# Four graph layers on one core: a shared pool of PSUM banks, seven units, scores in three row groups, low halves of P on GpSimd

## The reference, cut to what matters

```
x = layernorm(x + L0(x, adj))   # 12-head attention, scores + beta*adj, masked where adj is 0
x = layernorm(x + L1(x, adj))   # 2 inner layers: u = h (W h)^T for two W, exp, times adj, @ (h W_lin), layernorm, relu
x = layernorm(x + L2(x, adj))   # 2 inner layers: softmax(h h^T) * adj, three projections, upper/diagonal/lower, layernorm, relu
x = layernorm(x + L3(x, adj))   # 12-head attention with adj as bias, then an output projection
# attention: P = softmax(q k^T * scale + bias) per head of 32 columns, out = P v
```

## Time and profile before

| what | value |
|---|---|
| median of 3 runs | 3090.86 us (3088.84 to 3092.55) |
| the profiled execution, its own time | 3095.68 us |
| span of its trace, first to last instruction | 3093.9 us |
| mean granted clock of PE | 0.979 of full speed |
| PE busy | 2961.7 us, 96%, 35008 matmuls (547 a unit) |
| DVE / ACT / POOL busy | 2503.8 / 1833.4 / 1129.4 us |

### The profile page before, as it was taken

One profiled execution on the slowest core, in us unless ns is written; L12 is line 12 of the kernel. 1 busy time (PEld: TensorE's weight loads), 2 busy tenths in 40 slices (PEclk: granted clock), 3 DMA queues, 4 the chain that ended last, 5 costly groups with the idle time before them and its releaser, 6 DMA issues.

```text
span 3093.9 us, 91346 instructions
## 1 busy us (share of the span) xinstructions
PE 2961.7 (96%) x35008; PEld 2240.0 (72%) x35008; DVE 2503.8 (81%) x8824; ACT 1833.4 (59%) x4885; POOL 1129.4 (37%) x2315
## 2 busy tenths in 40 slices
PE   3799999999999999999999999999999999999985
PEld 2677777777777777777777777777777777777753
DVE  5578888888888888888888888888888888888763
ACT  5456566666566666666656656666666665666542
POOL 1233333343343333334334334333333433333321
PEclk7899999999999999999999999999999999999996
DMA  7233443444444444444444434434444434443322
GB/s 212 49 61 70 77 80 74 75 80 79 70 80 80 69 80 77 71 81 79 72 75 80 79 71 81 79 68 81 78 74 78 78 73 75 80 77 72 65 50 44
DMA packets 804111, 237.84 MB, mean 77 GB/s; under 512 B 771552, under 2 KB 803424, under 8 KB 803552
## 3 DMA queue, kind: packets, MB, share of 16 engines
q1 hardware_dynamic: 796336, 219.42, 39.4%
q10 hardware_dynamic: 7344, 12.58, 1.3%
HBM read 30.54 MB, written 12.58 MB: 14 GB/s over the span
## 4 chain that ended last, share of the span: by engine, by line
PE 88%; DMA 6%; DVE 2%; ACT 2%; POOL 1%; issue 1%; SPq 1%; POOLq 0%; DVEq 0%; ACTq 0%
PE bank L575 11%; PE bank L577 10%; PE bank L576 10%; PE bank L630 8%; PE bank L563 8%; PE bank L565 8%; PE bank L564 8%; PE bank L681 7%; DMA turned<-flat 5%; PE bank L581 3%; PE bank L613 3%; PE bank L676 3%; PE bank L614 2%; PE bank L615 2%; PE bank L645 1%; PE bank L647 1%
## 5 line engine op out<-in xcount | busy, mean ns | idle before, releaser
L563 PE MATMUL bank<-turned,w_hi 128*128 128x128 f16 x4608 | 821.4, 220 | 12.8 <-DVE ab L744 5.1
L565 PE MATMUL bank<-turned,w_lo 128*128 128x128 f16 x4608 | 821.8, 221 | 0.0
L564 PE MATMUL bank<-turned,w_hi 128*128 128x128 f16 x4608 | 821.8, 221 | 0.0
L506 ACT ACTIVATE ab<-bank 128x384 f16<-128x384 f32 (+1 forms) x896 | 436.6, 487 | 636.0 <-PE bank L581 240.7
L575 PE MATMUL bank<-w_hi,turned 128*128 128x384 f16 x2112 | 693.1, 328 | 25.2 <-DMA turned<-flat 23.5
L576 PE MATMUL bank<-w_lo,turned 128*128 128x384 f16 x2112 | 692.9, 328 | 0.0
L577 PE MATMUL bank<-w_hi,turned 128*128 128x384 f16 x2112 | 692.9, 328 | 0.0
L515 ACT ACTIVATE score<-score,small 128x128 f32<-128x128 f32 x1536 | 499.9, 392 | 91.0 <-DVE small L760 73.6
L744 DVE SCALAR_TENSOR_TENSOR ab<-bank,ab 128x384 f16<-128x384 f32 x512 | 276.8, 550 | 251.0 <-ACT ab L506 251.0
L563 PEld LDWEIGHTS bank<-turned,w_hi 128*128 128x128 f16 x4608 | 457.8, 99 | 29.2 <-issue 15.6
L564 PEld LDWEIGHTS bank<-turned,w_hi 128*128 128x128 f16 x4608 | 454.2, 99 | 14.4 <-issue 0.2
(11 more groups left out here) (118 smaller groups left out, 6503.0 us busy)
## 6 DMA issues: line engine op xcount, KB each, us to landing
turned<-flat SPq DMA_TRANSPOSE x960, 2.8
x<-x_dram SPq DMA_DIRECT2D x64, 192.0 KB, 2.6
out_dram<-score SPq DMA_DIRECT2D x64, 192.0 KB, 2.2
adj<-adj_dram SPq DMA_DIRECT2D x64, 64.0 KB, 2.4
z<-w_dram ACTq DMA_DIRECT2D x6, 576.0 KB, 4.3
score<-w_dram ACTq DMA_DIRECT2D x6, 576.0 KB, 6.1
mask<-w_dram ACTq DMA_DIRECT2D x6, 576.0 KB, 4.2
rows<-rows_dram ACTq DMA_DIRECT2D x1, 1920.0 KB, 8.4
```

The lines of the kernel that those rows point to most:

```text
L506: act.activation(dst, src, ACT.Copy, scale=scale / WSCALE).then_inc(proj_hi_done.of(i), 1)
L563: pe.matmul(dst, lhsT=w_hi[:, w, k, cols], rhs=t_hi[u][:, k, :], start=(k == 0), stop=False)
L564: pe.matmul(dst, lhsT=w_hi[:, w, k, cols], rhs=t_lo[u][:, k, :], start=False, stop=False)
L565: last = pe.matmul(dst, lhsT=w_lo[:, w, k, cols], rhs=t_hi[u][:, k, :], start=False, stop=(k == DT - 1 and w not in BIAS_OF))
```

## The change

- **Scores in three row groups and banks.** The weights Q and K of L0 and L3 are permuted on the host (`skewed`), so that in round `g` tile `t` uses rows of group `(g + t) % 4`; each tile goes to a bank of its own, and the nine matmuls run tile by tile within each of the three products.
- **A pool of banks.** The eight banks belong to no unit. `plan()` gives every PE step one bank (three to `scores`) when it lists the step, and the step waits (`bank_is_read`) for the step that reads the bank's last content. The waits of a unit's projections for each other go.
- **Seven units** in flight; the memory of the eighth pays for weight stages and a last column (`flat` is 385 wide, and L1's third projection goes there).
- **A planned order.** `plan()` places steps greedily: each engine takes, of the steps that are ready by the costs of the table `PARTS`, the one with the least wanted time, unit `i` shifted by `i * 41.768`. The order differs from unit to unit. The first x is loaded ahead of the weights.
- **P's low halves on POOL**: `scores_lo` on DVE goes, and POOL gets a step `scores` with the same subtraction.

```diff
-UNITS = 8
+UNITS = 7
+BANKS = 8
-PERIOD = UNITS * 44.578
-TIMES = {
-    ("scores_lo", 0): {VECTOR: 31.47},
...
+PERIOD = 41.768
+PARTS = {
+    (PE, "scores", 0): (21.14, 0.280, 0.460, ((VECTOR, "project", 0), (VECTOR, "project", 1), (VECTOR, "project", 2)), ()),
+    (POOL, "scores", 0): (47.71, 0.980, 1.050, ((SCALAR, "scores", 0),), ()),
...
+        now, engine, chosen = best
...
+        if engine == PE:
+            taken = [b for _, b in freed[:BANKS_OF.get(part[1], 1)]]
+            banks[part[1], part[2], i] = taken, [holder[b] for b in taken]
+            for b in taken:
+                holder[b] = READ_BY[part[1]](part[2]), i
...
+            def bank_is_read(i, name, k):
+                for holder in BANKS_AT[name, k, i][1]:
+                    if holder is None:
+                        continue
+                    (_, read_by, n), j = holder
+                    if read_by == "project":
+                        pe.wait_ge(*(proj_hi_done if READ_BY["project"](n)[0] == SCALAR else proj_lo_done).at(j, "made", n))
+                    elif read_by == "scores":
+                        pe.wait_ge(*topped.at(j, DT - 1, n))
...
             def scores(i, s):
-                head = slice(HD * g, HD * g + HD)
-                for t in range(DT):
-                    for qp, kp, n in ((a_hi, b_hi, 0), (a_hi, b_lo, 1), (a_lo, b_hi, 2)):
-                        last = pe.matmul(banks[u][:, t * N:(t + 1) * N], lhsT=qp[u][head, t, :], rhs=kp[u][head, t, :],
+                bank_is_read(i, "scores", s)
+                for qp, kp, n in ((a_hi, b_hi, 0), (a_hi, b_lo, 1), (a_lo, b_hi, 2)):
+                    for t in range(DT):
+                        group = (g + t) % HG
+                        head = slice(HD * group, HD * group + HD)
+                        last = pe.matmul(bank("scores", s, i, t)[:, 0:N], lhsT=qp[u][head, t, :], rhs=kp[u][head, t, :],
...
+            def scores(i, s):
+                pool.wait_ge(*cast.at(i, "p", s))
+                pool.tensor_tensor(flat[u][:, 1, :], score_at[u], flat[u][:, 0, :], ALU.subtract).then_inc(low_made.of(i), 1)
...
-            def scores_lo(i, s):
-                dve.wait_ge(*cast.at(i, "p", s))
-                dve.tensor_tensor(flat[u][:, 1, :], score_at[u], flat[u][:, 0, :], ALU.subtract).then_inc(mixed_out.of(i), 1)
```

More of the change, by code:

```diff
@@ L134 @@
 }
-START = [2.0 + i * PERIOD / UNITS for i in range(B)]
 STAGES = 3
@@ L142 @@
 PLACE = {w: n for n, w in enumerate(WEIGHT_ORDER)}
-EARLY = 3
-WEIGHT_TIMES = {w: START[0] + (2.0 * n if n < EARLY else 8.0 + 5.2 * (n - EARLY)) for n, w in enumerate(WEIGHT_ORDER)}
-STAGES_FREE = max(WEIGHT_TIMES.values()) + 3.0
-LENT = 4
-assert STAGES_FREE + 1.0 < START[LENT]
-assert all(t + 1.0 < START[0] + TIMES["project", w][PE] for w, t in WEIGHT_TIMES.items())
-def sequence(engine):
-    at = [(START[i] + t[engine], name, k, i) for (name, k), t in TIMES.items() if engine in t for i in range(B)]
-    if engine in (SCALAR, VECTOR):
-        at += [(t + (engine == VECTOR), "weight", w, 0) for w, t in WEIGHT_TIMES.items()]
-        at.append((WEIGHT_TIMES[WEIGHT_ORDER[1]] - 0.5 + (engine == VECTOR), "biases", 0, 0))
-        at.append((STAGES_FREE, "stages_free", 0, 0))
-    return [step[1:] for step in sorted(at)]
+WEIGHTS_FROM, WEIGHT_EVERY, LOAD_EVERY = 5.5, 4.4, 10.0
@@ L162, with first @@
+BANKS_OF = {"scores": DT}
+WEIGHT_COST = {("weight", SCALAR): 1.1, ("weight", VECTOR): 1.3, ("biases", SCALAR): 1.1, ("biases", VECTOR): 2.2}
+ORDER, BANKS_AT = plan()
+def sequence(engine):
+    return ORDER[engine]
+def first(engine, name, *numbers):
+    return next((k, i) for n, k, i in sequence(engine) if n == name and (not numbers or k in numbers))
 class Signal:
@@ L186, in per_unit @@
         def per_unit(name, shape, dt=F32):
[L188 to L189 removed]
+            return [sb(f"{name}_{u}", shape, dt)[:, :] for u in range(UNITS)]
         def sem(name):
@@ L755, in scores @@
                 if g:
-                    dve.wait_ge(*mixed_out.at(i, "low p", s - 1))
+                    dve.wait_ge(*low_made.at(i, "p", s - 1))
                 dve.wait_ge(*attending.at(i, "scored", s))
                 for t in range(DT):
-                    dve.tensor_tensor_reduce(out=score[u][:, t, :], in0=banks[u][:, t * N:(t + 1) * N],
+                    dve.tensor_tensor_reduce(out=score[u][:, t, :], in0=bank("scores", s, i, t)[:, 0:N],
                                              in1=(mask_bias if s < HG else minus_adj)[u], scale=1.0, scalar=BIG,
@@ L898 @@
     biases += [a["L3_gnn_bv"]]
+    skewed = _np.array([(HG * t + (group - t) % HG) * HD + c for t in range(DT) for group in range(HG) for c in range(HD)])
+    for w in (L0_Q, L0_K, L3_Q, L3_K):
+        ws[w] = ws[w][:, skewed]
+    for b in (BIAS_OF[L0_Q], BIAS_OF[L0_K]):
+        biases[b] = biases[b][skewed]
     rows = []
```

563 lines of the change are left out of this document (359 added, 204 removed).

## The result

| kernel | median us | runs us |
|---|---|---|
| before | 3090.15 | 3088.84 to 3092.55 |
| changed | 3041.86 | 3039.71 to 3042.03 |

The ratio is 0.9841, 95% interval [0.9821, 0.986]: 48 us faster. The forecast was 121 us faster. So the direction and the range held; the size did not. (A fourth execution of the changed kernel took 5084.74 us at a granted clock of 0.567; the median counts it, the ratio does not, and without it the median is 3041.7.)

What follows compares the result with a forecast made beforehand. PE's own work bounds the middle, and the ends lose 164 us. From 3095.7: scores -128, groups +16, ends -45, middle +35, median -4.8, giving 2970 us, 3.9% faster; range 2900 to 3100, the forecast's own 2915 to 3025.

Steps and rivals of the forecast that it cites:

- Scores, 128 us, with 16 for the groups: Score matmuls on PE: nine take 0.25 us less by overlapping, 128 us gained; 78 more score groups cost 16 us.
- The better bound: Score matmuls on PE: each triple costs what one matmul costs, a gain of 171 us.
- Rival C: Score matmuls on PE: the row groups don't overlap, 3097 us, no change or just slower; chance 0.08.
- the estimate that I drew from 81 ns for a pair: Score matmuls on PE: at the skill's pace per load and matmul, nine pairs could not go below 0.73 us.
- Low halves on POOL, "no price of its own": P's subtraction moved from DVE to POOL: a unit's path grows 2.9 us, covered by other units' matmuls, so nothing charged.
- Rival B: DVE and POOL shut each other out on SBUF, DVE sets the pace: slower, 3113 us; chance 0.13.
- Ends, 45 us less: Start and drain of the run: 30 of 72 us lost come back, and 15 of 88; bounds 0 and 80.
- Middle, 35 us more, bounds 0 and 84: Middle of the run: seven units leave 16% less room and the order is irregular, so some steps come late.
- the 3% of one window: Kernel before, 165 to 300 us, four to six units begun: 1567 matmuls where the middle's pace gives 1613.
- rival A: Middle and ends: the order starves PE more often, the ends give nothing, still faster, 3020 to 3080 us; chance 0.15.
- What would show it: Signs listed for the changed profile: score step time, matmuls per window, PE's busy share, low half on POOL, stretched DVE instructions.
- my own criterion: PE in the changed profile: waiting more than 1.5 us a unit for transposes would mean rival A.

## Why the prediction was right in sign and wrong in size

**What bounds the kernel** was right: PE in the middle. Going back to one row group costs 109 and, in the old order, 95 us, though no other engine's work changes.

**Scores, 128 us, with 16 for the groups:** the mechanism was right and the size too small. I took 0.25 us for nine matmuls from `attend`'s pace of 25 ns a pair. A triple costs about what one costs: in the records of single matmuls the three start 3 to 6 ns apart, and the next three 49 to 60 ns after them. From the step's start to the start of a next step of another kind the median is 0.276 us against 0.607 before. In the changed kernel's own order, with one row group or with three, PE's work differs by 163 us. Against the kernel before all score steps together take 135 us instead of 299, and going in costs 8 more for the added groups: 157 us net of the 166, where I had 112. The better bound, 171 less the 16 of the groups, was met. How much of it arrives depends on what else PE waits for: 95 to 109 us in two experiments. Rival C falls with it, and with C the estimate that I drew from 81 ns for a pair. A rule that I had not weighed fits: the Trainium skill (TensorE: Matmul & The Clock Gate, Part 3: Packing small matmuls, The mechanism) has tiles in different row groups start about 4 ns apart; the trace agrees, by 3 to 6 ns.

**Low halves on POOL, "no price of its own":** wrong, though by little in this order. The duration was right (0.95 us against 0.92). The step that failed is the inference that a lengthened path costs nothing while no row of PE's waits names it: in this order it costs 17 to 30 us, and in the old one, whose lists were made without it, 270. Rival B's exclusion is there, as the durations of L993, which was L813, show:

```profile
L993 DVE CUSTOM_DVE_ANT_0 score<-score,adj x128: 257/286/1093, 158.3 to 2966.1; 128x128 f32<-128x128 f32 x128
```

But the median is what it was, and DVE is 79% busy in the middle, not 90%, so B as a bound falls.

**Ends, 45 us less:** the difference was 8. The start gained 17 instead of 30, in part because `bias_x` at the head of POOL's list waited 18.9 us for the table of rows. With that wait gone the first window gets back 7 of the 13 us that are missing; the other 6 stay open. I had said that the early loads were covered by the wait for the first weight; that holds for PE, not for POOL's list. The window from 165 to 300, where I had nothing, lost 19 more: it looks as if the middle's loss has already begun there. The drain gave 10 of 15.

**Middle, 35 us more, bounds 0 and 84:** the step that failed, with 119. I scaled the loss with the number of units in flight and took the window at 165 to 300 us of the kernel before as the worst case. But with eight units the planned order still lost 138 us, and the old order in its place ran 68 us faster. So the loss comes mainly with the order: the same instructions in another draw of the greedy plan move it by tens of microseconds, and all eight plans lie above my bound, the best just above. What part, if any, is owed to seven units instead of eight stays open, since single plans differ by more. Nothing in the diff or in the trace of the kernel before told how good a new list would be; the 3% of one window was no bound for it. This is **rival A** in its size (3020 to 3080) and in its first half, PE starved more often by late transposes; its reason, longer paths with seven units, has only a small part shown: in the same order the short and the one-input low halves gave 30 and 17 us back.

**What would show it:** score step 0.35 with the way out (0.27); 547 matmuls in 44 to 45 us (2520 / 30398 x 547 = 45.3); PE 97 to 99% in the middle (2446 / 2520 = 97.1%); 1470 matmuls in 165 us (1401); waits for transposes above 1.5 us a unit would mean A. PE's idle time in the middle is 2520 - 2446 = 74 us in 55.6 units, 1.3 us a unit with all releasers, so by my own criterion A would not have been met. The loss of 130 us is larger than this idle time, and the records of single matmuls say where the rest is. Of the 115 us that remain when going in to the scores is counted as work, 90 lie in 128 steps with an idle stretch (74 idle, 16 beside it, covered by the spans of matmuls in the pipeline), and 24 in steps without one, most of it the slower clock.

**Still open:** which property makes one list lose 85 and another 176 us. Spare time in the plan was tried once and didn't help. That the tuned shift gives the best of three in all three rows of the table says that the tables were fitted together with it, and this is argued, not shown.

## What to carry to other kernels

A kernel whose engines run fixed lists has a price for the list itself; here a shift of 0.1 us in the planner, with no instruction changed, moved the time by 43 to 86 us, as much as the whole change or more. So compare an edit within one order, and where it must be planned anew, take several neighbouring plans before anything is put down to the edit. Small matmuls of K = 32 in different row groups and banks are worth having (163 us of PE's work here, in one order), but how much of it arrives depends on the list: the best kernel, 2978 us, is the old list with the row groups and the bank pool.

## What the hardware showed that I had not expected

- Three matmuls of 32 x 128 in three row groups and banks start 3 to 6 ns apart and together cost about what one costs, 55 ns, though each brings its own weight load.
- A wait of PE can cost more than its length: behind 0.84 and 1.79 us of idleness, 3.4 us of matmuls ran at half pace, at a granted clock of 0.75 for the window of 5 us.
- How much the exclusion between POOL and DVE depends on POOL's own inputs: with one SBUF input instead of two (and 256 columns instead of 384, 886 against 950 ns), DVE's busy time fell by 56 us in the same order, and the L1030s that start beside POOL's low half last 619 ns instead of 1039.
